# First recurrent step of a two-layer network: gate guards and learning rates moved to GpSimd, a series for the later rates

## The reference, cut to what matters

```python
ga = (2 * (ga >= 0) - 1) * maximum(abs(ga), 0.25)
```

```python
q, k, v = silu(h @ W_qkv)            # q, k then divided by their norms
lr = softplus(h @ W_lr + b_lr + log(expm1(0.01)))   # 3 rates per token and head
for each chunk:
    gate, hb, dhidden = k @ w0, k @ w2, v @ w1.T
    w1g, w0g, w2g = newtonschulz5 of the three gradients (two steps, bf16)
    w_i = (w_i + w_ig) / (norm(w_i + w_ig) + 1e-5) * norm(w_i at the start)
    o = silu(q @ w0) * (q @ w2) @ w1
out = (o / rms(o) * onorm_w) @ W_proj
```

## Time and profile before

| what | us |
|---|---|
| median of 3 runs | 1015.84 (1014.73 to 1016.3) |
| the profiled execution | 1013.95 |
| its span in the trace | 1011.9 |
| recurrence, steps 0 to 7, with the start | the first 400, roughly |
| the rest (feed-forward, layer 1) | the other 612 |
| DVE between 24 and 54 of the span | 24.2 busy of 30 |
| GpSimd between 73 and 87 of the span | 0.0 busy of 14 |

### The profile page before, as it was taken

The page is one execution under the profiler, slowest core; times in us unless marked ns, Lnnn a source line. Parts: engine busy times, 40 slices in busy tenths (PEclk is TensorE's granted clock), DMA queues, the critical chain, the costliest instruction groups (busy, mean ns, idle before and its releaser), DMA issues.

```text
span 1011.9 us, 24653 instructions
## 1 busy us (share of the span) xinstructions
PE 954.8 (94%) x9502; PEld 718.5 (71%) x9502; DVE 695.5 (69%) x2072; ACT 576.7 (57%) x1537; POOL 435.5 (43%) x391
## 2 busy tenths in 40 slices
PE   5887999999999999999999999999999999999988
PEld 3565887887886755666556769786878687868646
DVE  4889989989989942213222577876787678777884
ACT  2667888888888852222214275655565556555541
POOL 1320240340532711101011666775677567779720
PEclk9999999999999999999999999999999999999999
DMA  9250000000000001900001422222222222212202
GB/s 312 74 197 3 2 0 0 0 0 0 0 2 2 2 1 30 344 11 1 1 0 42 91 58 54 68 60 53 53 65 64 53 54 63 64 38 48 95 3 85
DMA packets 32811, 52.94 MB, mean 52 GB/s; under 512 B 7760, under 2 KB 17744, under 8 KB 31824
## 3 DMA queue, kind: packets, MB, share of 16 engines
q1 hardware_dynamic: 32720, 51.69, 18.5%
HBM read 22.57 MB, written 2.10 MB: 24 GB/s over the span
## 4 chain that ended last, share of the span: by engine, by line
PE 46%; DVE 8%; ACT 2%; issue 2%; POOL 1%; DMA 0%; SPq 0%; DVEq 0%; POOLq 0%
PE quad L2151 9%; PE quad L1740 8%; PE quad L2110 8%; PE quad L2054 5%; PE quad L2170 5%; PE quad L2184 4%; DVE act_probs L2509 2%; DVE wq_wo L2524 2%; PE quad L2248 1%; DVE x_pairs L2541 1%; ACT act_probs L2407 1%; PE quad L2118 1%; PE quad L1626 1%; PE quad L2073 1%; ACT hT L1639 1%
## 5 line engine op out<-in xcount | busy, mean ns | idle before, releaser
L2763 POOL TENSOR_TENSOR act_probs<-act_probs,rden 128x512 f32<-128x512 f32 (+3 forms) x128 | 169.3, 1329 | 103.3 <-DVE rden L2529 103.3
L2407 ACT ACTIVATE act_probs<-act_probs,neg_max 128x256 f32<-128x256 f32 (+3 forms) x256 | 141.1, 553 | 84.5 <-DVE neg_max L2509 84.1
L2110 PEld LDWEIGHTS quad<-hT,ug_queries 128*128 128x128 f32 x1024 | 122.6, 192 | 14.4 <-issue 7.7
L2110 PE MATMUL quad<-hT,ug_queries 128*128 128x128 f32 x1024 | 124.7, 275 | 1.2 <-ACT act_probs L2417 0.5
L1740 PE MATMUL quad<-hT,ug_raw_switch 128*128 128x512 f32 x256 | 113.9, 595 | 0.0
L1755 DVE SCALAR_TENSOR_TENSOR act_probs<-quad,ws_up,silu_keys 128x512 f32<-128x512 f32 x32 | 24.0, 750 | 98.2 <-ACT silu_keys L1750 98.2
L1750 ACT ACTIVATE silu_keys<-quad,ws_gate 128x512 f32<-128x512 f32 x32 | 22.0, 688 | 118.6 <-PE quad L1740 118.6
L1740 PEld LDWEIGHTS quad<-hT,ug_raw_switch 128*128 128x128 f32 x256 | 47.5, 190 | 54.9 <-issue 54.8
L2151 PE MATMUL quad<-down_raw_out,ug_raw_switch 128*128 128x256 f32 (+3 forms) x256 | 79.6, 439 | 4.7 <-DVE neg_max L2509 4.7
L2151 PE MATMUL quad<-silu_keys,ug_raw_switch 128*128 128x256 f32 (+3 forms) x256 | 79.6, 439 | 3.7 <-DVE neg_max L2509 3.7
L2529 DVE RECIPROCAL rden<-den 128x2 f32<-128x2 f32 x128 | 20.2, 158 | 82.9 <-ACT act_probs L2407 82.7
(11 more groups left out here) (339 smaller groups left out, 2309.8 us busy)
## 6 DMA issues: line engine op xcount, KB each, us to landing
rope_swapped<-gate SPq DMA_DIRECT2D x120, 64.0 KB, 2.0
ug_raw_switch<-gate SPq DMA_DIRECT2D x60, 128.0 KB, 2.3
ug_raw_switch<-in_wmod SPq DMA_DIRECT2D x4, 512.0 KB, 7.1
x_pairs<-in_x SPq DMA_DIRECT2D x4, 512.0 KB, 7.5
x_rows<-x_pairs SPq DMA_DIRECT2D x8, 256.0 KB, 5.0
wq_wo<-in_wq_nopeT SPq DMA_DIRECT2D x1, 2048.0 KB, 8.6
wq_wo<-in_wo SPq DMA_DIRECT2D x1, 2048.0 KB, 13.1
ug_queries<-in_switch_w SPq DMA_DIRECT2D x1, 2048.0 KB, 8.1
```

The costliest lines, as they stand in the source:

```text
L2110: mm = nc.tensor.matmul(out[:, P * i:P * i + P], w[:, kt, HP * half + i, :], in_order(k.hT[:, kt, b, cols], i), start=(kt == 0), stop=(kt ...
L2407: nc.scalar.activation(tile, tile, ACT.Exp, bias=neg_max[:, r, e:e + 1], scale=-1.0, accum_out=den[:, r, e:e + 1])\
L2763: nc.gpsimd.tensor_tensor(tile, tile, rden[:, t % RING, :].unsqueeze(2).to_broadcast([P, 2, cols]), ALU.mult)\
```

## The change

- `guard_gates` runs on GpSimd, for both layers, behind GpSimd's step 0 and before its step 1. Without the fused two-operand form it is five instructions a layer and not four, each waiting for the one before. SP's spreads wait for five counts a layer.
- The learning rates need no Ln. `one_more` and `logarithm` go, `ratio` (two DVE instructions) comes, and `finish` evaluates the series: 10 fused instructions on DVE for part 0, 17 on GpSimd for part 1, there behind the `hid` instructions of step 1. Their scratch moves from `hid_o` to `add`.
- ACT's Exp for part 1 moves from between the copies of YT to behind `root_state(0)` at the end of step 0. The reload of the Sqrt table goes.
- `normalize` of group 3 and the scaling of the projection weights go to GpSimd, behind `hid` of step 0. `scale_signs` goes to GpSimd, late in the recurrence (before step 6).
- `start_sums` is cut in three and moved ahead: two sums before each of the two `square_qk(0, i)` and two behind the normalization of group 2. Its wait for the state loads (`w_in`) moves with it.

The core of the diff:

```diff
@@ -190,19 +190,22 @@
...
 
-    def guard_gates(self, dve, l):
-        v, at = self.k.nc.vector, slice(2 * self.ROWS, 4 * self.ROWS)
+    def guard_gates(self, pool, l):
+        g, at, n = self.k.nc.gpsimd, slice(2 * self.ROWS, 4 * self.ROWS), 5 * l
         raw, sign, size = (x[at, :] for x in (self.rows[l], self.sign, self.size))
-        dve.wait_ge(self.rows_taken, l + 1)
-        dve.wait_ge(self.turned, l + 1)
+        pool.wait_ge(self.rows_taken, l + 1)
+        pool.wait_ge(self.turned, l + 1)
         if l == 1:
-            dve.wait_ge(self.step, 4)
-        v.tensor_scalar(sign, raw, 0.0, 2.0, ALU.is_ge, ALU.mult).then_inc(self.step, 1)
-        v.scalar_tensor_tensor(size, raw, -1.0, raw, ALU.mult, ALU.max).then_inc(self.step, 1)
-        dve.wait_ge(self.step, 4 * l + 2)
-        v.tensor_scalar(size, size, 0.25, None, ALU.max).then_inc(self.step, 1)
-        dve.wait_ge(self.step, 4 * l + 3)
-        v.scalar_tensor_tensor(raw, sign, -1.0, size, ALU.add, ALU.mult).then_inc(self.step, 1)
+            pool.wait_ge(self.step, 5)
+        g.tensor_scalar(sign, raw, 0.0, 2.0, ALU.is_ge, ALU.mult).then_inc(self.step, 1)
+        pool.wait_ge(self.step, n + 1)
+        g.tensor_scalar(sign, sign, -1.0, None, ALU.add).then_inc(self.step, 1)
+        pool.wait_ge(self.step, n + 2)
+        g.tensor_tensor(size, raw, sign, ALU.mult).then_inc(self.step, 1)
+        pool.wait_ge(self.step, n + 3)
+        g.tensor_scalar(size, size, 0.25, None, ALU.max).then_inc(self.step, 1)
+        pool.wait_ge(self.step, n + 4)
+        g.tensor_tensor(raw, sign, size, ALU.mult).then_inc(self.step, 1)
 
     def row(self, l, half, b, n):
@@ -211,7 +214,7 @@
...
     def spread(self, sp, l):
         k = self.k
-        sp.wait_ge(self.step, 4 * l + 4)
+        sp.wait_ge(self.step, 5 * l + 5)
         for b in range(B):
@@ -256,11 +259,13 @@
...
 
-    def normalize(self, dve, g):
-        dve.wait_ge(self.rstd_done, g + 1)
+    def normalize(self, eng, by, g):
+        eng.wait_ge(self.rstd_done, g + 1)
+        if g == 3:
+            eng.wait_ge(self.xn_done, 4 * g)
         for v, x in enumerate(self.tiles(g)):
             n = 4 * g + v
-            self.k.nc.vector.tensor_scalar(self.xn[g][:, v, :], x, self.mv[:, n, 0:1], self.rstd[:, n:n + 1],
+            by.tensor_scalar(self.xn[g][:, v, :], x, self.mv[:, n, 0:1], self.rstd[:, n:n + 1],
                                            ALU.subtract, ALU.mult).then_inc(self.xn_done, 1)
...
     def turn(self, pe, g, kt, out):
@@ -301,7 +306,8 @@
...
     SPLIT = 4 * R
-    OPS = 12
+    OPS = 14
+    TERMS = 7
 
     def __init__(self, k, scope, spare, rows):
@@ -356,11 +362,6 @@
...
         self.k.nc.scalar.activation(v, u, ACT.Exp).then_inc(self.lr_act, 1)
-
-    def logarithm(self, act, part):
-        z, u, v, m, lr = self.columns(part)
-        act.wait_ge(self.step, self.OPS * part + 3)
-        self.k.nc.scalar.activation(u, m, ACT.Ln).then_inc(self.lr_act, 1)
 
     def start(self, dve, part):
@@ -376,31 +377,37 @@
...
 
-    def one_more(self, dve, part):
+    def ratio(self, dve, part):
         z, u, v, m, lr = self.columns(part)
-        dve.wait_ge(self.lr_act, 2 * part + 1)
-        self.k.nc.vector.tensor_scalar(m, v, 1.0, None, ALU.add).then_inc(self.step, 1)
-
-    def finish(self, dve, part):
-        nc = self.k.nc
+        dve.wait_ge(self.lr_act, part + 1)
+        self.k.nc.vector.tensor_scalar(u, v, 2.0, None, ALU.add).then_inc(self.step, 1)
+        dve.wait_ge(self.step, self.OPS * part + 3)
+        self.k.nc.vector.reciprocal(u, u).then_inc(self.step, 1)
+
+    def finish(self, eng, by, part, fused):
         z, u, v, m, lr = self.columns(part)
-        n = [self.OPS * part + 3]
+        n = [self.OPS * part + 4]
 
         def done(op):
...
             op.then_inc(self.step, 1)
-            dve.wait_ge(self.step, n[0])
-
-        dve.wait_ge(self.lr_act, 2 * part + 2)
-        done(nc.vector.tensor_scalar(m, m, -1.0, None, ALU.add))
-        done(nc.vector.tensor_tensor(u, u, v, ALU.mult))
-        done(nc.vector.tensor_scalar(lr, m, 0.0, None, ALU.is_equal))
-        done(nc.vector.tensor_tensor(v, v, lr, ALU.mult))
-        done(nc.vector.tensor_scalar(m, m, 1e-30, None, ALU.max))
-        done(nc.vector.reciprocal(m, m))
-        done(nc.vector.tensor_tensor(u, u, m, ALU.mult))
-        done(nc.vector.tensor_tensor(u, u, v, ALU.add))
-        done(nc.vector.scalar_tensor_tensor(lr, z, 0.0, u, ALU.max, ALU.add))
+            eng.wait_ge(self.step, n[0])
+        eng.wait_ge(self.step, n[0])
+        done(by.tensor_tensor(m, v, u, ALU.mult))
+        done(by.tensor_tensor(v, m, m, ALU.mult))
+        done(by.tensor_scalar(u, v, 2.0 / (2 * self.TERMS - 1), None, ALU.mult))
+        for term in range(self.TERMS - 2, -1, -1):
+            by_what = v if term else m
+            if not fused:
+                done(by.tensor_scalar(u, u, 2.0 / (2 * term + 1), None, ALU.add))
+                done(by.tensor_tensor(u, u, by_what, ALU.mult))
+            else:
+                done(by.scalar_tensor_tensor(u, u, 2.0 / (2 * term + 1), by_what, ALU.add, ALU.mult))
+        if fused:
+            done(by.scalar_tensor_tensor(lr, z, 0.0, u, ALU.max, ALU.add))
+        else:
+            done(by.tensor_scalar(m, z, 0.0, None, ALU.max))
+            done(by.tensor_tensor(lr, m, u, ALU.add))
 
...
 def stage_fast_weights(k):
@@ -484,7 +491,7 @@
...
         mods, first_norm = Modulations(k, scope, spare=oT[:].rearrange("p i h c -> p (i h c)")), StartNorm(k, scope)
-        rates = LearningRates(k, scope, spare=hid_o[:].rearrange("p i h c -> p (i h c)"), rows=h_o)
+        rates = LearningRates(k, scope, spare=add[:].rearrange("p i d -> p (i d)")[:, D // 2:], rows=h_o)
         w_in, qkv_in, proj_in, n0_step = (k.sem(n) for n in ("fw_state_in", "fw_qkv_in", "fw_proj_in", "fw_start_step"))
@@ -1042,17 +1049,12 @@
...
                             rates.take_rest(act)
-                        elif n == 6:
-                            rates.exponential(act, 1)
                     elif ph == A1:
...
                     ffn.take_fold(act, 4, bank[FOLD_BANK[4]])
-                if first:
-                    rates.logarithm(act, 1)
-                    load_table(ACT.Sqrt)
 
                 def square_state(q):
@@ -1080,6 +1082,8 @@
...
                 root_state(0)
+                if first:
+                    rates.exponential(act, 1)
                 load_table(ACT.Silu)
@@ -1122,7 +1126,6 @@
...
             take_qk(0, 1, 3)
-            rates.logarithm(act, 0)
             load_table(ACT.Silu)
@@ -1211,13 +1214,13 @@
...
 
-            def start_sums():
+            def start_sums(m):
                 dve.wait_ge(w_in, STATE_IN)
-                for m in range(3):
-                    for hd in range(H):
-                        op = nc.vector.tensor_tensor_reduce(n0_sq[:, H * m + hd], state[:, m, hd, :], state[:, m, hd, :], 1.0, 0.0, ALU.mult, ALU.add,
-                                                            n0_rows[:, H * m + hd:H * m + hd + 1])
-                op.then_inc(n0_step, 1)
+                for hd in range(H):
+                    op = nc.vector.tensor_tensor_reduce(n0_sq[:, H * m + hd], state[:, m, hd, :], state[:, m, hd, :], 1.0, 0.0, ALU.mult, ALU.add,
+                                                        n0_rows[:, H * m + hd:H * m + hd + 1])
+                if m == 2:
+                    op.then_inc(n0_step, 1)
 
             def start_norms():
@@ -1251,8 +1254,6 @@
...
                     square_qk(1, 0, (0, 1, 2, 3))
-                    start_sums()
-                    first_norm.normalize(dve, 3)
                 for n, q in enumerate(MQ):
@@ -1268,7 +1269,6 @@
...
                     square_qk(1, 1, (0, 1, 2, 3))
-                    mods.guard_gates(dve, 0)
                 elif not more:
@@ -1299,16 +1299,12 @@
...
                         first_norm.modulate_half(dve, 3, bank[6])
-                if first:
-                    mods.guard_gates(dve, 1)
                 for n, q in enumerate(NQ):
...
                         rates.start(dve, 1)
-                if first:
-                    rates.one_more(dve, 1)
 
                 def update(q):
@@ -1368,30 +1364,29 @@
...
             first_norm.sums(dve, 1)
-            first_norm.normalize(dve, 0)
-            first_norm.normalize(dve, 1)
+            first_norm.normalize(dve, nc.vector, 0)
+            first_norm.normalize(dve, nc.vector, 1)
             dve.wait_ge(mods.taken, 2)
...
             for i in range(PAIRS):
+                start_sums(i)
                 dve.wait_ge(s["qkv_acted"], i + 1)
...
             rates.start(dve, 0)
-            first_norm.normalize(dve, 2)
+            first_norm.normalize(dve, nc.vector, 2)
+            start_sums(2)
             norm_qk(0)
...
             scale_first(0)
-            rates.one_more(dve, 0)
+            rates.ratio(dve, 0)
             scale_first(1)
             first_norm.sums(dve, 3)
```

(26 more changed lines are left out.)

## The result

The kernel after takes 1007.24 us (median; 1007.09 to 1009.7) beside 1016.06 (1014.73 to 1016.3): ratio 0.9922, interval 0.9904 to 0.9939, a gain of 8.8. Forecast: 1008.0. Its profiled execution took 1007.32, span 1005.5, against 1013.95 and 1011.9: 6.4 of span. Both sizes have to be explained, so I read the trace by milestones first and the whole times last.

The account below looks back on a forecast made before the run. The prediction read the recurrence as stages each released by the one before, so savings in step 0 and into step 1 reach the end whole: 0.25 + 3.65 + 2.45 + 1.5 = 7.85, 1015.84 - 7.85 = 1008.0 us, range 1004.8 to 1012.3.

Parts of the forecast that it names:

- start: DVE's queue to the end of the part-0 rates: the Ln wait goes, a state-load stall replaces it; gain 0.25.
- middle: Step 0 up to the gradient norm: state sums, normalization and layer 0's guard leave DVE's path; gain 3.65, guard 2.24.
- end: End of step 0 to the first factor: Exp and table loads no longer delay it, guard 1 counts nothing; gain 2.45.
- turn: Way into step 1: 2.8 from rate instructions, scale, signs and clock, less 1.0 at the gates and 0.3 collisions; gain 1.5.
- rival 2: Step 0 is DVE's throughout, so guard 1 counts too and collisions do not: gain 10.4, 1005.4 us; chance 0.12.
- the guards meet DVE at work that reads PSUM: GpSimd's guards, counted at about 9 us, run beside DVE instructions reading PSUM; their work was counted at nothing.
- The first factor near 79.8: Sign that the forecast is right: in step 0 the first factor comes near 79.8 us.
- updates starting before 71: Sign against the forecast: state updates of step 0 starting before 71 us would point to rival 2.
- The clock stays: At the weight transposes into step 1, PE's idle shrinks to some 1.8 and the granted clock stays at 1.0.
- GpSimd's prices: Assumed costs of moved work: 0.65 per 512-column scaling, 0.35 per 256 columns, 0.25 per 72-column series instruction (17, 4.3 together).
- Rival 3: GpSimd's series is late before `scale_qk` in step 1; 1.13 per instruction takes back all 7.85, 1.3 gives 1018.8; chance 0.06.
- Rival 1: GpSimd's moved instructions hold DVE's, at step 0's squares of G and in step 1: gain 4.1, 1011.7 us; chance 0.12.

Follow-up runs that it names:

- same: The kernel after, run once more unchanged, beside the kernel before: 1005.30 us, ratio 0.9876.
- e3_guards: Kernel after with both layers' guards back on DVE at their old places: 1011.52 us, ratio 0.994 to the kernel before.
- e2_guard1: Kernel after with only layer 1's guard back on DVE, behind the Y scalings; layer 0's stays on GpSimd: 1009.68 us, ratio 0.9932 to the kernel before.
- e4_exp: Kernel after with ACT's part-1 Exp back between the copies of YT and the Sqrt table reload restored: 1010.88 us, ratio 0.9936 to the kernel before.
- norm_back: Kernel after with group 3's normalization and the projection's scale back on DVE: 1009.79 us, ratio 0.992 to the kernel before.
- e8_clock: Kernel after plus six unread 128x512 TensorE products ahead of the updated weights' transposes in step 0: 1009.87 us, ratio 0.9934 to the kernel before.
- e6_prices: Kernel after plus six unread 128x256 GpSimd instructions of different kinds ahead of step 1's `hid`: 1010.53 us (one run).
- e5_twice: Kernel after with group 3's norm done a second time on GpSimd into scratch, in step 0: 1010.69 us (one run).
- e7_longer: Kernel after with one 72-column maximum of GpSimd's series done 13 times instead of once: 1010.51 us (one run).

## Why the prediction was right

The number was right (1008.0; range 1004.8 to 1012.3), and the forecast case was the one that happened. That it came within 1 is in part luck: in the trace of after two disturbances took back 2.3 of an 8.4 that the undisturbed program has, and the same program once more has a median of 1005.30. Gains summed up to each milestone, before to after and before to same:

| step of the prediction | cumulated | after | same |
|---|---|---|---|
| start, 0.25 | 0.25 | 0.75 | 0.54 |
| middle, 3.65 | 3.90 | 3.57 | 4.61 |
| end, 2.45 | 6.35 | 4.34 | 6.67 |
| turn, 1.5 | 7.85 | 6.12 | 8.44 |

- **Start.** Right: loads at 25.9 (forecast 26.0), the wait for them (2.33) in place of the one for Ln. From the first state sum to the end of the rates it took 10.5, where the sum had 10.9; the other 0.1 is that the loads landed at 25.9.
- **Middle.** The guard is right (2.24 forecast, 2.32 measured). The other 1.4 I put down to sums and norm added up; there is a slack of 1.27 behind them, so one of the two alone costs 0.45 or nothing, and both cost 1.75.
- **End.** Right that guard 1 is free (rival 2 falls, by e3_guards, and by e2_guard1, where only the stretching cost) and that the Exp is what is late: back in its place it costs 1.11. Wrong in "the guards meet DVE at work that reads PSUM": the row of 72.73 runs on into the squares of the state, because the guards took 15.9, not 9. Cost 1.1 where it hits (1.3 with the held instruction of the rates before it), 0 where it misses by a few tenths, and in after it hit. "The first factor near 79.8" was my own slip: 82.43 less 6.35 is 76.1, and same has it at 75.76. By the same slip "updates starting before 71" was no sign of rival 2: the forecast itself has 72.95 less 3.9, so 69.05, and they started at 70.03 in after and 68.74 in same.
- **Turn.** The size is right (1.78 gained in after, 1.5 forecast), and so is the 1.0 that ScalarE takes back: 17.17 against 16.15 undisturbed, with TensorE waiting 0.96 for the weight copy. That undoing the Exp's move gives it back isn't shown: in e4_exp the clock fell in its place. "The clock stays" holds in same (idle 1.80), not in after (3.10, which is the 1.8 and the 1.3 of the end), and "ScalarE's lateness covers it" holds in both. Of what left DVE here only the projection's scale was put back alone (norm_back, 0.55, the scale together with the norm); that the nine rate instructions are the rest is by the sum, not by a run.
- **GpSimd's prices** are the terms that I had wrong throughout, without an effect on the time: a 256-column scaling with two scalars out of tiles 1.42, not 0.35; 512 columns 1.57, not 0.65; the 17 short ones 8.4, not 4.3. I had taken the copy for the nearest row. No cover broke, since each was two to four times the wrong sum. That was luck, since no row had shown such a scaling; the series came within 2.5 of the path. Rival 3 needed 1.13 each and got 0.49.
- **Rival 1**, the exclusion: its mechanism is real, its place was another. The Trainium skill (SBUF — State Buffer, "Who interferes with whom") has DVE and GpSimd lock each other out for whole instructions; the square of 72.84, let through when the guard instruction ends, agrees. Three squares of same that began in the middle of GpSimd's scaling of 70.49 took 0.29 and do not, and there the measurement decides: only beside a product of two tensors was a square of the state held until the end. Of the two places that I had named, DVE shows an idle of 1.23 to 1.27 behind the squares of G, and the last four of these took 1.42 as in before (1.41); in step 1 of same it waited 0.78 ahead of them, and the same four took 1.63.

## What to carry to other kernels

Work moved off a busy engine is free only if its cover holds at the price of the new engine, and afterwards it matters beside what it runs: put it next to instructions that read PSUM, and keep products of two tensors away from runs of short ones that read SBUF. Two pieces taken from the same engine ahead of one wait do not add up; undo each alone before crediting either. Run the kernel itself again before crediting an experiment with a microsecond, and compare distances between milestones, because a clock that falls elsewhere is worth as much.

## What the runs showed of the hardware

- One program gave two traces whose middles differ by 1.25, with the clock at 34 to 40 (0.72 or 1.00; TensorE idle 1.23 or 0.92 ahead of it), and ends that differ by 1.29, of which a single square of 1.35 in place of 0.28 is 1.07. The phase of GpSimd against DVE that decides this square is a few tenths: in e8_clock the same guard instruction began at 73.09, 0.04 behind the last square of its group, and held none.
- Eight of DVE's squares of step 0's state began inside one of GpSimd's products of two 64x512 tensors: 1.35 long in after, norm_back and e6_prices, 0.47 and 1.34 in e5_twice, 1.17 in e4_exp, 0.32 in same, 0.34 in e7_longer. All ended 0.14 to 0.15 behind the product's end. Those that began inside one of its instructions on one tensor took 0.28 or 0.29, or 0.45 and 0.69 (e5_twice).
- GpSimd ran a plain scaling with a constant (0.89 for 256 columns) slower than a product of two tensors (0.72) or a copy (0.51), beside the same busy DVE.
- Instructions of 72 columns cost GpSimd 0.34 to 0.58 each, 8.4 for 17 with what lies between them.
